# A macaron block on one core: the second expert layer as three 128-column products into the same PSUM columns

## The chip, the core and the metric

The kernel runs on one core of one Trainium2 chip. The time is that of one execution in microseconds (us); the runs of the kernel before gave 599.95, 600.19 and 601.44, median 600.19.
## The reference

For 8192 tokens of 128 numbers: a routed feed-forward layer, a gated scan over 512 steps, and the feed-forward layer again. The routed layer is

```
h = jnp.mod(x_flat[:, :TOP_K].sum(axis=1).astype(jnp.int32), E)
sel = jnp.stack([h, jnp.mod(h + 1, E)], axis=1)
def step(acc, params):
    e, W1e, b1e, W2e, b2e = params
    w = jnp.any(sel == e, axis=1).astype(x.dtype) / TOP_K
    y = jnp.maximum(x_flat @ W1e + b1e, 0.0) @ W2e + b2e
    return (acc + w[:, None] * y, None)
...
x = x + 0.5 * _L0_ffn_ref(_layernorm(x, axis=-1), L0_ffn_W1, L0_ffn_b1, L0_ffn_W2, L0_ffn_b2)
```

With E = 8 experts each token goes to its class's expert and the next one. W1 is 128 x 512 and W2 512 x 128 for each expert.

## The kernel before, in words

`ffn(r)` runs twice (r = 0 and 1), with the scan layer between. Each time, the tokens have been sorted by class, so that a tile of 256 tokens is gathered by two indirect DMAs and written back by two (the last tile has 128). There are 36 tiles per call. 25 are **pure**: all 256 tokens have one class. 11 are **mixed**: their two sub-blocks of 128 tokens may have different classes, so each has its own experts. The program has the order fixed: three pure tiles, then eleven times two pure and one mixed (`layout`).

- `layer1(tile, e)`, lines 745 to 759: for the expert e of two, four chunks of three matmuls. In a pure tile they have 256 columns, in a mixed tile each chunk is done twice with 128. The weights are the operand that is loaded into the array, `hi` and `lo`: two register adds for three matmuls.
- `layer2(tile, e)`, lines 761 to 779: for each chunk c and sub-block s, `hhi` (the high part of the hidden layer) is loaded and the columns `w` stream past it: 256, which are the weight's high and low half side by side. Then `hlo` is loaded, and `wh`, the high half, streams with 128. So Y has 256 columns per sub-block: the second half holds high x low. Both matmuls read the same register.
- `step(tile)`, lines 781 to 803: PE's order per iteration is layer1 of tile j for e = 0, the transposes of tile j + 1, layer2 of tile j - 1 for e = 0, layer1 of j for e = 1, layer2 of j - 1 for e = 1. In the last iteration that has a tile, layer1 for e = 1 comes ahead of layer2.
- `collect(tile)` on DVE, lines 1063 to 1070: O += scale x Y's first half, then, behind the semaphore `y_half`, O += scale x Y's second half. It stands behind `low` (lines 1043 to 1049), which makes the hidden layer's low part from ACT's high part (line 586).
- POOL gathers four tiles ahead and scatters three tiles behind (lines 498 to 509). Its scatters wait for `o_ready` of the collecting operation.

Of the kernel before, what the change touches and what calls it, by code (L numbers as in the profile page):

```python
# [17 lines left out]
ALU = mybir.AluOpType  # L18
# [4 lines left out]
P = 128  # L23
# [3 lines left out]
def macaron_kernel(nc, x, W_toP, W_U, W_F, W_V, W_lam, B_mat, C_mat, W_fromP, W1, b1, W2, b2, out):  # L27
# [6 lines left out]
    FT = 256  # L34
    SUB = FT // P
# [22 lines left out]
    with ExitStack() as ctx:  # L58
# [3 lines left out]
        def sem(name):  # L62
            return ctx.enter_context(nc.semaphore(name))
# [6 lines left out]

        ps = ctx.enter_context(nc.psum_tensor("ps", [P, 8, 512], F32))
        H = [ps[:, 2 * e:2 * e + 2, :].rearrange("p a (b n) -> p (a b) n", n=FT) for e in range(2)]
        Y = [ps[:, 4 + k, :].rearrange("p (s n) -> p s n", s=SUB) for k in range(2)]
        XTP = ps[:, 6, 0:FT]

# [25 lines left out]
        scl = scl_i[:].bitcast(F32)  # L102
# [58 lines left out]
        hhi = [[sb(f"hhi{k}{e}", [P, CH, FT], F16) for e in range(2)] for k in range(2)]  # L161
        hlo = [[sb(f"hlo{k}{e}", [P, CH, FT], F16) for e in range(2)] for k in range(2)]
# [82 lines left out]
        lo_done = [sem(f"lo_done{e}") for e in range(2)]  # L245
        res_done = sem("res_done")
        y_ready = sem("y_ready")
        y_half = sem("y_half")
        o_ready = sem("o_ready")
        scat = [sem(f"scat{k}") for k in range(SLOTS)]  # L250
        mxn0 = sem("mxn0")
# [413 lines left out]
        def _(pe):  # L665
# [74 lines left out]
            def ffn(r):  # L740
                load, held = table(PE_E, tab_w[:].rearrange("p j e -> p (j e)"), 2 * SUB, (E - 1) * WS), {}
                w1v = w1s[:].rearrange("p e f -> p (e f)")
                w2v = w2s[:].rearrange("p e c f -> p (e c f)")

                def layer1(tile, e):

                    pe.wait_ge(xlo_ready, tile.done())
                    if tile.j >= 1:
                        pe.wait_ge(lo_done[e], (tile + -1).done())
                    for s in range(1 if tile.pure else tile.subs):  # L750
                        at, tok = held[tile.j][2 * s + e], slice(0, FT) if tile.pure else slice(s * P, (s + 1) * P)
                        for c in range(CH):
                            hi = w1v[:, bass.ds(at + c * P, P)]
                            lo = w1v[:, bass.ds(at + DFF + c * P, P)]
                            o = H[e][:, c, tok]
                            nc.tensor.matmul(o, hi, xhi[tile.k][:, tok], start=True, stop=False)  # L756
                            nc.tensor.matmul(o, hi, xlo[tile.k][:, tok], start=False, stop=False)  # L757
                            ins = nc.tensor.matmul(o, lo, xhi[tile.k][:, tok], start=False, stop=True)  # L758
                    ins.then_inc(h_ready[e], 1)

                def layer2(tile, e):

                    pe.wait_ge(lo_done[e], tile.done())
                    if tile.r == 0 and tile.j == 0 and e == 0:
                        pe.wait_ge(w2_split, 2)
                    if e == 0 and tile.j >= 2:
                        pe.wait_ge(o_ready, (tile + -2).done())
                    for c in range(CH):
                        for s in range(tile.subs):
                            at, tok = held[tile.j][e if tile.pure else 2 * s + e], slice(s * P, (s + 1) * P)  # L770
                            w = w2v[:, bass.ds(at + c * 2 * P, 2 * P)]
                            wh = w2v[:, bass.ds(at + c * 2 * P, P)]
                            first = e == 0 and c == 0 and s == 0
                            nc.tensor.matmul(Y[tile.k][:, s, :], hhi[tile.k][e][:, c, tok], w,  # L774
                                             start=first, stop=False, skip_group_check=True)
                            ins = nc.tensor.matmul(Y[tile.k][:, s, 0:P], hlo[tile.k][e][:, c, tok], wh, start=False,  # L776
                                                   stop=(e == 1 and c == CH - 1), skip_group_check=True)
                    if e == 1:
                        ins.then_inc(y_ready, 1)

                def step(tile):
                    now, nxt, was = tile.valid(), (tile + 1).valid(), tile.j >= 1

                    early = tile.j == NJ - 1
                    if now:
                        layer1(tile, 0)
                    if nxt:
                        pe.wait_ge(xn_ready, (tile + 1).done())
                        if tile.j >= 0:
                            pe.wait_ge(xlo_ready, tile.done())  # L790
                        for s in range((tile + 1).subs):
                            ins = nc.tensor.transpose(XTP[:, s * P:(s + 1) * P], xn[(tile + 1).k][:, s, :], ident[:])  # L792
                        ins.then_inc(xt_ready, 1)
                    if tile.j == -1:
                        warm(5)
                    if early:
                        layer1(tile, 1)
                    if was:
                        layer2(tile + -1, 0)
                    if now and not early:  # L800
                        layer1(tile, 1)
                    if was:
                        layer2(tile + -1, 1)

                pe.wait_ge(table_ready, 1 + r)
                for j in range(-1, NJ + 1):
                    if 0 <= j < NJ:
                        held[j] = load(Tile(r, j).at)
                    step(Tile(r, j))
                    held.pop(j - 1, None)  # L810
# [68 lines left out]
        def _(dve):  # L879
            v = nc.vector  # L880
# [153 lines left out]
            def ffn(r):  # L1034
                load = table(DVE_E, tab_b2[:], SUB, (E - 1) * D)
                b2v = b2t[:].rearrange("p e d -> p (e d)")

                def x_low(tile):
                    dve.wait_ge(xhi_ready, tile.done())
                    c = slice(0, tile.cols)  # L1040
                    v.tensor_tensor(xlo[tile.k][:, c], XTP[:, c], xhi[tile.k][:, c], ALU.subtract).then_inc(xlo_ready, 1)  # L1041

                def low(tile, e):

                    dve.wait_ge(hi_done[e], tile.done())
                    c = slice(0, tile.cols)
                    v.scalar_tensor_tensor(out=hlo[tile.k][e][:, :, c], in0=H[e][:, :, c], scalar=0.0,  # L1047
                                           in1=hhi[tile.k][e][:, :, c], op0=ALU.max,
                                           op1=ALU.subtract).then_inc(lo_done[e], 1)

                def residual(tile):
                    at = load(tile.at)
                    if r == 0 and tile.j == 0:
                        dve.wait_ge(b2_ready, 1)
                    dve.wait_ge(gath[tile.slot], tile.moved())
                    if tile.j >= SLOTS:
                        dve.wait_ge(scat[tile.slot], (tile + -SLOTS).moved())
                    for s in range(tile.subs):
                        ins = v.tensor_tensor(O[tile.slot][:, s, :], G[tile.slot][:, s, 0:D],  # L1059
                                              b2v[:, bass.ds(at[0 if tile.pure else s], D)], ALU.add)  # L1060
                    ins.then_inc(res_done, 1)

                def collect(tile):
                    o, y = O[tile.slot][:, 0:tile.subs, :], Y[tile.k][:, 0:tile.subs, :]
                    dve.wait_ge(y_ready, tile.done())
                    v.scalar_tensor_tensor(out=o, in0=y[:, :, 0:P], scalar=scl[:, 2:3], in1=o, op0=ALU.mult,  # L1066
                                           op1=ALU.add).then_inc(y_half, 1)
                    dve.wait_ge(y_half, tile.done())
                    v.scalar_tensor_tensor(out=o, in0=y[:, :, P:2 * P], scalar=scl[:, 2:3], in1=o,  # L1069
                                           op0=ALU.mult, op1=ALU.add).then_inc(o_ready, 1)  # L1070

                x_low(Tile(r, 0))
                if r == 0:
                    w2_low(1)
                for j in range(NJ):
                    tile = Tile(r, j)
                    low(tile, 0)
                    if j + 1 < NJ:
                        x_low(tile + 1)
                    residual(tile)  # L1080
                    low(tile, 1)
                    if j >= 1:
                        collect(tile + -1)
                collect(Tile(r, NJ - 1))

            ffn(0)
# [119 lines left out]
```

## Time and profile before

| | |
|---|---|
| median of the runs | 600.19 us (599.95 to 601.44) |
| the profiled execution, first to last instruction (span) | 598.6 us |
| first call of ffn, about 61.5 to 262.6 us | 201 us |
| second call, about 385.5 to 584.7 us, and its last scatters | 199 us, and 14 us |
| PE busy | 514.1 us, 86% of the span |
| DVE busy | 432.9 us, 72% |

Of the profiled execution the page gives the span; its lowest run is 1.4 us longer, for what lies around the program. Matmuls are pipelined, and a matmul's row gives its own duration, longer than its place in the stream; what a matmul costs in a stream is the distance between the starts of two that follow each other. Sequencer rows are not counted as busy time, and PE's are listed only where a line of the program is asked for.

### The profile page before, as it was taken

The numbers are of one execution on the slowest core, as the hardware profiler recorded it, in microseconds if no ns is written. First come the engines' busy times: TensorE is split into PE (matmuls) and PEld (weight loads), VectorE is DVE, ScalarE is ACT, GpSimd is POOL, SyncE is SP. The second block draws the span as 40 slices with busy tenths as digits, with TensorE's granted clock in tenths as the row PEclk, the third lists the DMA queues.
The fourth block names the chain that finished last, engine by engine and source line by source line (L and its number), as shares of the span: only waits on it lengthen the run. The fifth ranks groups of instructions, "written<-read, shape, count | busy, mean of one in ns | idle before, by whom it ended". The sixth has DMA issues, their size and how long they took to land.

```text
span 598.6 us, 15962 instructions
## 1 busy us (share of the span) xinstructions
PE 514.1 (86%) x5269; PEld 437.2 (73%) x5269; DVE 432.9 (72%) x1026; ACT 296.2 (49%) x494; POOL 321.1 (54%) x410
## 2 busy tenths in 40 slices
PE   0278899999999999956799836999999999999990
PEld 0136599999999999942466614689999999999980
DVE  6899677777777777746876779677777777777760
ACT  2384655555555556412988400155555655555540
POOL 3014847777777767350016610447777677777543
PEclk9996999999999999997999967699999999999996
DMA  9980111112111112109003380111121111112100
GB/s 244 328 340 11 41 34 50 47 47 50 48 51 43 51 41 53 31 30 266 16 1 72 72 142 1 28 38 46 51 50 48 44 46 47 48 51 51 36 24 18
DMA packets 37850, 40.96 MB, mean 68 GB/s; under 512 B 5813, under 2 KB 30731, under 8 KB 37266
## 3 DMA queue, kind: packets, MB, share of 16 engines
q1 hardware_dynamic: 27698, 21.65, 13.5%
q0 software_dynamic: 9088, 17.87, 11.5%
q8 instruction: 51, 0.84, 0.6%
q10 hardware_dynamic: 992, 0.44, 0.3%
q14 instruction: 21, 0.17, 0.1%
HBM read 23.00 MB, written 17.83 MB: 68 GB/s over the span
## 4 chain that ended last, share of the span: by engine, by line
PE 69%; DVE 14%; issue 5%; DMA 3%; ACT 3%; POOL 3%; SPq 2%; POOLq 0%; DVEq 0%
PE ps L774 19%; PE ps L756 10%; PE ps L758 10%; PE ps L757 10%; PE ps L776 10%; PE ps L792 2%; SPq L366 2%; PE ps L680 2%; PE ps L728 2%; DMA X<-in_L_attn_x 1%; DVE X L1122 1%; DVE bn L1101 1%; POOL G L478 1%; DVE onehot_b L987 1%; PE ps L836 1%
## 5 line engine op out<-in xcount | busy, mean ns | idle before, releaser
L1047 DVE SCALAR_TENSOR_TENSOR hlo<-ps,hhi 128x1024 f16<-128x1024 f32 x144 | 174.1, 1209 | 103.0 <-ACT hhi L586 103.0
L586 ACT ACTIVATE hhi<-ps 128x1024 f16<-128x1024 f32 x144 | 145.7, 1012 | 170.1 <-PE ps L758 170.1
L774 PE MATMUL ps<-w2s,hhi 128*128 x1136 | 202.3, 273 | 0.0
L776 PE MATMUL ps<-w2s,hlo 128*128 x1136 | 194.9, 219 | 0.0
L478 POOL DMA_INDIRECT G<-rows,places x142 | 141.9, 1000 | 88.2 <-issue 40.2
L756 PE MATMUL ps<-xhi,w1s 128*128 128x256 f16 (+1 forms) x736 | 168.0, 248 | 3.9 <-DVE xlo L1041 2.1
L758 PE MATMUL ps<-xhi,w1s 128*128 128x256 f16 (+1 forms) x736 | 168.0, 248 | 0.0
L757 PE MATMUL ps<-xlo,w1s 128*128 128x256 f16 (+1 forms) x736 | 167.9, 248 | 0.0
L774 PEld LDWEIGHTS ps<-w2s,hhi 128*128 128x128 f16 x1136 | 111.1, 98 | 12.1
L776 PEld LDWEIGHTS ps<-w2s,hlo 128*128 128x128 f16 x1136 | 111.1, 98 | 1.3
L486 POOL DMA_INDIRECT x1d<-O,places x71 | 71.3, 1004 | 41.6 <-issue 29.1
L486 POOL DMA_INDIRECT out<-O,places x71 | 71.3, 1004 | 40.3 <-issue 26.8
L600 ACT ACTIVATE xn<-G 128x127 f32<-128x127 f32 x142 | 62.0, 489 | 50.0 <-DMA G<-rows,places 50.0
L756 PEld LDWEIGHTS ps<-xhi,w1s 128*128 x736 | 72.0, 98 | 11.2 <-issue 6.0
L758 PEld LDWEIGHTS ps<-xhi,w1s 128*128 x736 | 72.0, 98 | 4.7
L757 PEld LDWEIGHTS ps<-xlo,w1s 128*128 x736 | 72.0, 98 | 3.4
L680 PE MATMUL ps<-ones_row,ones 128*128 128x512 f16 x111 | 32.7, 459 | 11.7 <-DMA X<-x1d 11.0
L1066 DVE SCALAR_TENSOR_TENSOR O<-ps,scl_i,O 128x256 f32<-128x256 f32 x72 | 34.0, 472 | 3.6 <-PE ps L776 3.6
L1069 DVE SCALAR_TENSOR_TENSOR O<-ps,scl_i,O 128x256 f32<-128x256 f32 x72 | 34.6, 481 | 2.5
L680 PEld LDWEIGHTS ps<-ones_row,ones 128*128 128x128 f16 x111 | 12.7, 116 | 29.6 <-issue 21.7
L1059 DVE TENSOR_TENSOR O<-G,b2t 128x128 f32<-128x128 f32 x142 | 34.3, 282 | 0.0
L1041 DVE TENSOR_TENSOR xlo<-ps,xhi 128x256 f16<-128x256 f32 x72 | 29.5, 410 | 2.6 <-ACT xhi L592 2.6
(240 smaller groups left out, 509.5 us busy)
## 6 DMA issues: line engine op xcount, KB each, us to landing
rows<-X SPq DMA_DIRECT2D x2, 2080.0 KB, 12.0
rows<-X SPq DMA_DIRECT2D x4, 1040.0 KB, 7.6
X<-in_L_attn_x SPq DMA_DIRECT2D x8, 512.0 KB, 8.0
X<-x1d SPq DMA_DIRECT2D x8, 512.0 KB, 7.4
G<-rows,places POOLq DMA_INDIRECT x142, 2.6
w1r<-in_L_ffn_W SPq DMA_DIRECT2D x1, 2048.0 KB, 11.3
x1d<-O,places POOLq DMA_INDIRECT x71, 2.3
out<-O,places POOLq DMA_INDIRECT x71, 2.3
```

The source lines that it names most:

```text
L478: nc.gpsimd.indirect_dma_start(out=G[tile.slot][:, s, :], out_offset=None, in_=rows, in_offset=bass.IndirectOffsetOnAxis(ap=places[:, tile ...
L486: nc.gpsimd.indirect_dma_start(out=dst, out_offset=bass.IndirectOffsetOnAxis(ap=places[:, tile.at, SUB + s:SUB + s + 1], axis=0), in_=O[ti ...
L586: nc.scalar.activation(hhi[tile.k][e][:, :, 0:tile.cols], H[e][:, :, 0:tile.cols], ACT.Relu).then_inc(hi_done[e], 1)
L600: ins = nc.scalar.activation(xn[tile.k][:, s, 0:D - 1], g[:, s, 0:D - 1], ACT.Identity, bias=g[:, s, D:D + 1], scale=g[:, s, D + 1:D + 2])
L680: nc.tensor.matmul(ps[:, bank, :], ones16[:], ones_row[:], start=True, stop=True)
L756: nc.tensor.matmul(o, hi, xhi[tile.k][:, tok], start=True, stop=False)
L757: nc.tensor.matmul(o, hi, xlo[tile.k][:, tok], start=False, stop=False)
L758: ins = nc.tensor.matmul(o, lo, xhi[tile.k][:, tok], start=False, stop=True)
L774: nc.tensor.matmul(Y[tile.k][:, s, :], hhi[tile.k][e][:, c, tok], w, start=first, stop=False, skip_group_check=True)
L776: ins = nc.tensor.matmul(Y[tile.k][:, s, 0:P], hlo[tile.k][e][:, c, tok], wh, start=False, stop=(e == 1 and c == CH - 1), skip_group_check ...
L1047: v.scalar_tensor_tensor(out=hlo[tile.k][e][:, :, c], in0=H[e][:, :, c], scalar=0.0, in1=hhi[tile.k][e][:, :, c], op0=ALU.max, op1=ALU.sub ...
L1069: v.scalar_tensor_tensor(out=o, in0=y[:, :, P:2 * P], scalar=scl[:, 2:3], in1=o, op0=ALU.mult, op1=ALU.add).then_inc(o_ready, 1)
```

## The change

`layer2` no longer streams 256 columns past `hhi`. It loads `hhi` and streams the high half (128 columns), loads `hlo` and streams the high half, loads `hhi` again and streams the low half. All three add into the same 128 columns, so Y has 128 columns per sub-block, and `collect` is one operation. `y_half` is gone.

```
-        Y = [ps[:, 4 + k, :].rearrange("p (s n) -> p s n", s=SUB) for k in range(2)]
+        Y = [ps[:, 4 + k, 0:FT].rearrange("p (s n) -> p s n", s=SUB) for k in range(2)]
...
-                            w = w2v[:, bass.ds(at + c * 2 * P, 2 * P)]
                             wh = w2v[:, bass.ds(at + c * 2 * P, P)]
+                            wl = w2v[:, bass.ds(at + c * 2 * P + P, P)]
                             first = e == 0 and c == 0 and s == 0
-                            nc.tensor.matmul(Y[tile.k][:, s, :], hhi[tile.k][e][:, c, tok], w,
-                                             start=first, stop=False, skip_group_check=True)
-                            ins = nc.tensor.matmul(Y[tile.k][:, s, 0:P], hlo[tile.k][e][:, c, tok], wh, start=False,
+                            y = Y[tile.k][:, s, :]
+                            nc.tensor.matmul(y, hhi[tile.k][e][:, c, tok], wh, start=first, stop=False,
+                                             skip_group_check=True)
+                            nc.tensor.matmul(y, hlo[tile.k][e][:, c, tok], wh, start=False, stop=False,
+                                             skip_group_check=True)
+                            ins = nc.tensor.matmul(y, hhi[tile.k][e][:, c, tok], wl, start=False,
                                                    stop=(e == 1 and c == CH - 1), skip_group_check=True)
...
-                    v.scalar_tensor_tensor(out=o, in0=y[:, :, 0:P], scalar=scl[:, 2:3], in1=o, op0=ALU.mult,
-                                           op1=ALU.add).then_inc(y_half, 1)
-                    dve.wait_ge(y_half, tile.done())
-                    v.scalar_tensor_tensor(out=o, in0=y[:, :, P:2 * P], scalar=scl[:, 2:3], in1=o,
-                                           op0=ALU.mult, op1=ALU.add).then_inc(o_ready, 1)
+                    v.scalar_tensor_tensor(out=o, in0=y, scalar=scl[:, 2:3], in1=o, op0=ALU.mult,
+                                           op1=ALU.add).then_inc(o_ready, 1)
```

PE, start of layer 2 of a mixed tile, in the kernel before. ps is PSUM, w2s the second layer's weights, and a MATMUL row stands for a weight load and a matmul:

```order
L792 MATMUL ps<-ident,xn 128x128 [waits xlo_ready,xn_ready]
L792 MATMUL ps<-ident,xn 128x128
L774 REGISTER_ALU [waits o_ready,lo_done0]
L774 MATMUL ps<-w2s,hhi 128x256
L776 MATMUL ps<-w2s,hlo 128x128
L774 REGISTER_ALU
```

The same place in the changed kernel:

```order
L794 MATMUL ps<-ident,xn 128x128 [waits xlo_ready,xn_ready]
L794 MATMUL ps<-ident,xn 128x128
L774 REGISTER_ALU [waits o_ready,lo_done0]
L774 MATMUL ps<-w2s,hhi 128x128
L776 MATMUL ps<-w2s,hlo 128x128
L778 REGISTER_ALU
L778 MATMUL ps<-w2s,hhi 128x128
L774 REGISTER_ALU
```

The third product's address has a register add of its own: two adds per chunk and sub-block where there was one.

PE, the first chunk of layer 2 of a pure tile, before, where both sub-blocks share the chunk's add:

```order
L774 REGISTER_ALU [waits o_ready,lo_done0]
L774 MATMUL ps<-w2s,hhi 128x256
L776 MATMUL ps<-w2s,hlo 128x128
L774 MATMUL ps<-w2s,hhi 128x256
L776 MATMUL ps<-w2s,hlo 128x128
L774 REGISTER_ALU
```

And now:

```order
L774 REGISTER_ALU [waits o_ready,lo_done0]
L774 MATMUL ps<-w2s,hhi 128x128
L776 MATMUL ps<-w2s,hlo 128x128
L778 REGISTER_ALU
L778 MATMUL ps<-w2s,hhi 128x128
L774 MATMUL ps<-w2s,hhi 128x128
L776 MATMUL ps<-w2s,hlo 128x128
L778 MATMUL ps<-w2s,hhi 128x128
L774 REGISTER_ALU
```

Here too each chunk has two adds for one. Over the program, layer 2's REGISTER_ALU rows go from 736 to 1472 and its matmuls (each with its load) from 2272 to 3408; the 1472 ISA rows of layer 1 and the waits on PE are as they were.

DVE, a tile's collecting operation between two `low`, before (O is the tile's output, scl the scale):

```order
L1047 SCALAR_TENSOR_TENSOR hlo<-ps,hhi 128x1024 [waits hi_done1]
L1066 SCALAR_TENSOR_TENSOR O<-ps,scl_i,O 128x256 [waits y_ready]
L1069 SCALAR_TENSOR_TENSOR O<-ps,scl_i,O 128x256 [waits y_half]
L1047 SCALAR_TENSOR_TENSOR hlo<-ps,hhi 128x1024 [waits hi_done0]
L1041 TENSOR_TENSOR xlo<-ps,xhi 128x256 [waits xhi_ready]
```

And now:

```order
L1049 SCALAR_TENSOR_TENSOR hlo<-ps,hhi 128x1024 [waits hi_done1]
L1068 SCALAR_TENSOR_TENSOR O<-ps,scl_i,O 128x256 [waits y_ready]
L1049 SCALAR_TENSOR_TENSOR hlo<-ps,hhi 128x1024 [waits hi_done0]
L1043 TENSOR_TENSOR xlo<-ps,xhi 128x256 [waits xhi_ready]
```

One of the two operations and the wait between them are gone; nothing else on DVE moved.

## Rows read from the trace of the kernel before

**Rows 1.** First section of the page: busy us (share of the span), instructions.

```profile
PE 514.1 (86%) x5269; PEld 437.2 (73%) x5269; DVE 432.9 (72%) x1026; ACT 296.2 (49%) x494; POOL 321.1 (54%) x410
```

**Rows 2.** Busy time by stretch (the two ffn calls), with the granted clock behind POOL.

```profile
61.50:264.50 203.00, 198.06 (x2317) 182.17 (x2316) 147.37 (x253) 109.78 (x178) 136.78 (x136) 1.00 0.17 44
386.50:585.00 198.50, 196.30 (x2311) 181.68 (x2309) 143.85 (x250) 108.57 (x176) 131.69 (x133) 1.00 0.17 45
```

**Rows 3.** Waits: who waited for whom, us in total, times, longest.

```profile
PE ps L756 <- DVE xlo L1041: 2.1, 2, 1.3
PE ps L756 <- DVE hlo L1047: 1.7, 3, 0.6
```

**Rows 4.** Groups by shape: count, busy us, mean ns of one, idle before.

```profile
L774 PE MATMUL ps<-w2s,hhi 128*128 x1136 | 202.3, 273 | 0.0
...
L1069 DVE SCALAR_TENSOR_TENSOR O<-ps,scl_i,O 128x256 f32<-128x256 f32 x70 | 33.9, 484 | 2.5
```

**Rows 5.** Timeline of PE, 202.5 to 209: start us, us; each stage's first matmul.

```profile
202.75 0.27 PE L774 MATMUL ps<-w2s,hhi 128*128 x1
...
204.07 0.27 PE L756 MATMUL ps<-xhi,w1s 128*128 128x256 f16 x1
...
205.38 0.27 PE L774 MATMUL ps<-w2s,hhi 128*128 x1
...
206.70 0.22 PE L756 MATMUL ps<-xhi,w1s 128*128 128x128 f16 x1
...
208.04 0.39 PE L792 MATMUL ps<-ident,xn 128*128 128x128 f32 x2
```

**Rows 6.** Timeline of weight loads, 579 to 580, first load of each chunk.

```profile
579.31 0.10 PEld L756 LDWEIGHTS ps<-xhi,w1s 128*128 x1 [0.74 <-issue]
...
579.56 0.10 PEld L756 LDWEIGHTS ps<-xhi,w1s 128*128 x1
...
579.80 0.10 PEld L756 LDWEIGHTS ps<-xhi,w1s 128*128 x1
```

**Rows 7.** Lines 774, 756, 304: sequencer rows, ns min/median/max, first to last start us.

```profile
L774 PEldq ALU_OP  x736: 32/32/42, 69.9 to 582.9; - x184
...
L756 PEldq FUSED_REGOPS  x736: 42/46/46, 62.9 to 580.1; - x184
...
L304 PEldq TENSOR_LOAD <-tab_w x72: 327/331/521, 61.6 to 576.4; - x72
```

**Rows 8.** Line 774, sequencer, 518.35 to 519.16: eight adds in a row.

```profile
L774 PEldq ALU_OP  x8: 32/32/32, 518.4 to 519.2; - x8
```

**Rows 9.** Lines 304, 749, 756, sequencer: the start of an iteration at 411.5.

```profile
L304 PEldq TENSOR_LOAD <-tab_w x1: 332/332/332, 411.5 to 411.5; - x1
...
L749 PEldq EVENT_SEMAPHORE  x1: 51/51/51, 411.9 to 411.9; - x1
...
L756 PEldq FUSED_REGOPS  x1: 42/42/42, 412.0 to 412.0; - x1
```

**Rows 10.** Line 756 and PE's timeline, 408.9 to 410.45: adds ahead of their matmuls.

```profile
L756 PEldq FUSED_REGOPS  x4: 42/46/46, 409.0 to 409.8; - x4
L756 PEld LDWEIGHTS ps<-xhi,w1s x1: 98/98/98, 410.3 to 410.3; 128*128 x1
...
409.06 0.27 PE L774 MATMUL ps<-w2s,hhi 128*128 x1
...
410.32 0.22 PE L776 MATMUL ps<-w2s,hlo 128*128 x1
```

**Rows 11.** Timelines of POOL and DVE at the end of the program.

```profile
581.40 0.98 POOL L486 DMA_INDIRECT out<-O,places  x1 [1.52 <-PE ps L758]
...
589.13 0.98 POOL L486 DMA_INDIRECT out<-O,places  x1 [0.31 <-issue]
...
585.08 0.35 DVE L1069 SCALAR_TENSOR_TENSOR O<-ps,scl_i,O 128x128 f32<-128x128 f32 x1
```

**Rows 12.** Busy time by stretch, in the scan layer; PE first, then PEld, DVE, ACT, POOL.

```profile
280.00:340.00 60.00, 54.60 (x349) 35.35 (x346) 45.63 (x190) 48.43 (x95) 19.22 (x68) 1.00 0.26 59
```

More of the change, by code:

```diff
@@ L247, in macaron_kernel @@
         y_ready = sem("y_ready")
-        y_half = sem("y_half")
         o_ready = sem("o_ready")
```

## The prediction

 The waits confirm it: over the program PE waits 3.8 us for DVE's low parts (2.1 + 1.7, five times) [rows 3], so DVE's 72% is not a limit. The ffn calls last as long as PE takes.
>
> What PE takes is the distance of matmul starts. The timeline gives three prices [rows 5]. Layer 2: 8 pairs (256 and 128 columns) from 202.75 to 204.07, 0.165 us a pair. Layer 1 of a pure tile: 12 matmuls of 256 columns from 204.07 to 205.38, 0.109 each. Layer 1 of a mixed tile: 24 matmuls of 128 columns from 206.70 to 208.04, 0.0558 each, every one with its own weight load. So loads are hidden behind 128 columns too.
>
> A second view has to be read, since PE's stream is fed by a sequencer that also does the register adds: 736 ALU_OP for layer 2, 1472 FUSED_REGOPS for layer 1 (736 for each of two lines), 72 TENSOR_LOADs [rows 7]. What an add takes there shows where nothing is queued. Near the end, after a wait, layer 1 of a mixed tile runs at one chunk per 0.245 us (579.31, .56, .80) [rows 6], though its three matmuls need 0.167. A chunk has two adds: **0.123 to 0.124 us per FUSED_REGOPS**. Its matmuls and loads add nothing visible. In layer 2 eight ALU_OPs stand in 0.8 us, seven steps: **0.114 us per ALU_OP** [rows 8], with two matmuls and their loads between. An iteration's TENSOR_LOAD and first wait take 0.5 us (411.5 to 412.0) [rows 9]; the other three waits 0.1 each, as the one from 411.9 to 412.0: 0.8 in all.
>
> This sequencer runs ahead, and a queue holds what it has handed over. How far: the adds of layer 1 run at 409.0, the load of the first of these matmuls at 410.3, and between them PE starts the 16 matmuls from 409.06 to 410.32 [rows 10]. I take 16 matmuls as the queue's depth.
>
> **The change part by part.**
>
> *Streamed columns.* As many as before (384), but in three matmuls: 3 x 0.0558 = 0.1674 against 0.165, so 0.0024 to 0.0026 more for each of 1136 groups [rows 4, 5]: **+2.9 us**, all on the path, since PE is it. That the three add into the same columns costs nothing: layer 1 of a mixed tile does the same at 0.0558.
>
> *One collecting operation less.* 0.48 us of DVE in each of 70 tiles, a bit less in two [rows 4]. What PE waits for on DVE is 3.8 us, at starts and ends of the calls [rows 3]; those waits end with `low` and `x_low`, at stage ends where `collect` comes behind them. At the program's end POOL's seven scatters, released by layer 1 of the last tile (581.40), follow each other to 589.13, while the last collecting operation starts at 585.08 [rows 11], 4 us ahead of the scatter that needs it; the first call ends alike. **0**, between 0 and -3.8.
>
> *Register adds.* 736 ALU_OPs more, one for `wl` per chunk (pure) or chunk and sub-block (mixed). They cost nothing while the sequencer keeps its lead. So the budget of a round of three tiles (two pure, one mixed), which the program repeats:
> - PE: layer 1 two pure tiles x 24 x 0.109 = 5.24, one mixed 48 x 0.0558 = 2.68; six transposes at a matmul's 0.109, 0.66; layer 2 three tiles x 16 x 0.1674 = 8.04 (before 7.92). **16.6 us** (before 16.5).
> - Sequencer: 16 + 16 + 32 = 64 FUSED_REGOPS x 0.124 = 7.94; ALU_OPs before 8 + 8 + 16 = 32 x 0.114 = 3.65, now 64, 7.30; three iterations x 0.8 = 2.4. Before **14.0**, now **17.6 us**.
>
> Before, the sequencer had 2.5 us to spare per round. Now it is 1.0 us short: it becomes the bound. Twice ten full rounds (the eleventh ends with the half tile) lose at least 20.4 us.
>
> More is lost, because lead beyond 16 matmuls (16 x 0.0558 = 0.89 us) can't be stored. I walk through a round, PE's time less the sequencer's, with L the lead. Layer 1 mixed: 1.34 - 1.98; pure: 1.31 - 0.99; layer 2 mixed: 1.34 - 1.82; pure: 1.34 - 0.91.
> - Mixed tile's layer 1, with the pure tile's layer 2. L = 0.89. e = 0: entry 0.5 and layer 1, -1.14: stall 0.25, L = 0; layer 2 +0.43. e = 1: -0.74: stall 0.31; +0.43.
> - Next, pure layer 1, mixed layer 2. e = 0: entry and layer 1 -0.18, L = 0.25; -0.48: stall 0.23. e = 1: +0.22, -0.48: stall 0.26, L = 0.
> - Then both pure. e = 0: entry 0.5 with nothing queued: stall 0.5; layer 1 +0.32, layer 2 +0.43. e = 1: +0.22, +0.43 makes 1.40, cut to 0.89.
>
> Sum 1.55 us per round, x 20 = **+31 us**. Bounds: 20 us if the lead is never cut. If ALU_OP's price is at the low end of what the rounded row allows (0.7 us for seven steps, 0.100), the round is short by 0.1 alone; with two thirds of the 0.5 us that the walk loses at the full queue that makes 0.45, 9 us. If a second add in a group costs as much as a FUSED_REGOPS, 0.124, a round loses 0.64 more: 44 us. I take 31, by the row that is the same operation in the same line.
>
> Sum: 2.9 + 0 + 31 = **+34 us** on a span of 598.6, and as much on the median 600.19: **634 us**.
>
> One page states a depth for this queue: the Trainium skill, "TensorE: Matmul & The Clock Gate", in its table ahead of the first section, gives TensorE 64 entries, which would be 32 matmuls with their loads; rows 10 show 16, and the measurement is what I go by. By the page's depth no lead is cut, and the sum is 2.9 + 20.4, 623 us.
>
> **The rivals.**
> - *The sequencer keeps up, and PE's stream alone decides.* So if the adds really overlap each other where matmuls are short. For it: no row before has two adds with a single matmul behind the second in layer 2. Against it: layer 1's chunk has exactly that pattern in rows 6, at 0.124 per add. It needs ALU_OP under (16.6 - 7.9 - 2.4) / 64 = 0.098. Then 600.2 + 2.9 = 603.1.
> - *Not slower: DVE's relief pays.* Same condition, under 0.098 per add, and then the 3.8 us of PE's waits for DVE [rows 3] must shrink, because `low` is issued half a microsecond earlier. At the most 600.2 + 2.9 - 3.8 = 599.3. Against it: these waits stand where no `collect` is ahead.
> - *Short matmuls with loads are slower than the rows say.* In a stream of load and matmul, 0.081 us each for 128 columns instead of 0.0558: 1136 x (3 x 0.081 - 0.165) = 88, 688 us. Against it: 24 in a row at 0.0558 [rows 5]. The figure is that of the Trainium skill, same page, section "Back-to-back issue gap"; this trace disagrees.
> - *The clock falls, since PE now stalls inside the stage.* One mixed tile at 1.2 GHz costs some 96 matmuls x 0.056 = 5 us, 20 of them 100 us: 734. Against it: the scan layer, where PE has gaps (54.6 of 60 us busy) [rows 12], keeps 1.00 from 280 to 340.
> - *The change doesn't do what it says*, the adds being shared: the order of the built program shows the 736 new ones. No chance.
>
> **How the numbers follow.** Sequencer-bound, 634: 0.85, of which 0.79 lies between 612 (9 + 2.9) and 648 (44 + 2.9). Deeper queue, 623: 0.04, inside as well. Stream alone, 603.1: 0.05. DVE's relief, 599.3: 0.04. Slow pairs 0.01, clock 0.01. Range 612 to 648, which holds 0.83. A measurement of this kernel can tell about 0.3%, 1.8 us: 603.1 is slower. Faster 0.02, the same 0.02 (the relief's two halves), slower 0.96.
>
> **What would show it.** ALU_OP of layer 2 1472 times, in mixed tiles with steps of about 0.11; layer 2 of a mixed tile no longer at 0.167 per group but towards 0.23, and layer 1 of a mixed tile towards 0.25 per chunk; a hole in PE of some 0.5 us at the start of the iteration behind a mixed tile's layer 2; both ffn calls longer by 15 to 19 us each and nothing else changed; the collecting operation at 0.48 us once per tile, DVE's busy time 36 us less; clock 1.00 in both calls. I am wrong if pure and mixed tiles alike run without holes (the adds are cheaper than I read), or if the third product's start is later than 0.056 behind the second in pure tiles too, where there is lead (a price of same columns or of loads).

## The result and the profile after

The changed kernel takes 651.06 us (649.71 to 651.08) beside 600.17 us (599.95 to 601.44) for the kernel before on the same chip: a ratio of 1.084, interval 1.0825 to 1.0856. It is slower, as forecast, but by 51 us instead of 34, and 3 us above the range.

The first section of its page (busy us, share of the span, instructions) answers to [rows 1]:

```profile
PE 556.5 (86%) x6405; PEld 468.4 (72%) x6405; DVE 398.7 (61%) x954; ACT 296.2 (46%) x494; POOL 321.4 (50%) x410
```

PE has 1136 matmuls more, DVE 72 operations and 34.2 us less. The span is 649.1 us, 50.5 more than before. The two ffn calls, which answer to [rows 2] (length, then PE, PEld, DVE, ACT, POOL, and behind them the granted clock):

```profile
61.50:289.10 227.60, 218.28 (x2886) 196.66 (x2884) 130.10 (x217) 109.75 (x178) 136.94 (x136) 1.00 0.15 40
...
411.00:637.00 226.00, 217.95 (x2885) 197.47 (x2884) 127.34 (x215) 108.93 (x178) 133.63 (x136) 1.00 0.16 40
```

Each call is longer by some 25 us (the forecast was 15 to 19), and the clock in both is 1.00 as before. PE counts as busy for 96% of either window (98 and 99% before), which looks like a PE that still sets the pace. It doesn't: a matmul's row lasts 0.22 us, so a next one that starts 0.1 us late leaves no idle time. Steps between starts have to be read, and the sequencer's rows. Those of layer 2 are at line 774 and at line 778, the third product, which the change gave an add of its own (count, ns min/median/max, first and last start):

```profile
L774 PEldq ALU_OP  x736: 32/32/42, 69.8 to 634.7; - x184
...
L778 PEldq ALU_OP  x736: 32/32/32, 70.0 to 634.8; - x184
```

So 1472 adds, as forecast. What they do to layer 2 of a mixed tile stands in the timeline of weight loads (start us, duration us), first load of each group:

```profile
504.24 0.10 PEld L774 LDWEIGHTS ps<-w2s,hhi 128*128 128x128 f16 x1
...
504.46 0.10 PEld L774 LDWEIGHTS ps<-w2s,hhi 128*128 128x128 f16 x1
...
504.69 0.10 PEld L774 LDWEIGHTS ps<-w2s,hhi 128*128 128x128 f16 x1
...
504.91 0.10 PEld L774 LDWEIGHTS ps<-w2s,hhi 128*128 128x128 f16 x1
...
505.19 0.10 PEld L774 LDWEIGHTS ps<-w2s,hhi 128*128 128x128 f16 x1
...
505.42 0.10 PEld L774 LDWEIGHTS ps<-w2s,hhi 128*128 128x128 f16 x1
```

A group takes 0.225 us, two adds at 0.113, where its three matmuls need 0.167. One step is 0.28 instead of 0.225: it holds a pause of about 0.055. That pause is what the prediction lacked.

The waits (who waited for whom, us in total, times, longest) have the two rows of [rows 3] unchanged, and a new one: twenty holes of 0.4 us at the start of an iteration, where layer 1's first matmul finds an empty queue. They hold 8 us of the loss; most of it stands in no row of waits.

```profile
PE ps L755 <- issue: 8.2, 20, 0.4
PE ps L755 <- DVE xlo L1043: 2.1, 2, 1.3
PE ps L755 <- DVE hlo L1049: 1.7, 3, 0.6
```

The length of a round of three tiles can be read from the table loads, one per iteration: 25 of them span eight rounds. Before, and then after (line, sequencer, operation, count, ns, first and last start):

```profile
L304 PEldq TENSOR_LOAD <-tab_w x25: 327/331/335, 428.0 to 560.0; - x25
```

```profile
L303 PEldq TENSOR_LOAD <-tab_w x25: 328/329/334, 456.9 to 608.6; - x25
```

132.0 / 8 = 16.50 us a round before, 151.7 / 8 = 18.96 after. Twenty rounds of 2.46 us are 49 of the 50.5 us.

### The profile page after: what moved, and what is told of

The parts are those of the page before. It is cut to its first block, busy times and chain, and to the rows that moved or that the text cites. A ratio compares the mean times of both kernels' runs of the same rounds, so it can differ in the third digit from the quotient of the medians.

```text
span 649.1 us, 18898 instructions
## 1 busy us (share of the span) xinstructions
PE 556.5 (86%) x6405; PEld 468.4 (72%) x6405; DVE 398.7 (61%) x954; ACT 296.2 (46%) x494; POOL 321.4 (50%) x410
## 4 chain that ended last, share of the span: by engine, by line
PE 71%; DVE 13%; issue 5%; DMA 3%; ACT 3%; POOL 2%; SPq 2%; POOLq 0%; DVEq 0%
PE ps L755 13%; PE ps L774 11%; PE ps L757 10%; PE ps L778 10%; PE ps L776 10%; PE ps L756 9%; PE ps L794 3%; SPq L365 2%; PE ps L727 1%; PE ps L679 1%; DMA X<-in_L_attn_x 1%; DVE X L1121 1%; DVE bn L1100 1%; POOL G L477 1%; DVE onehot_b L989 1%
## 5 line engine op out<-in xcount | busy, mean ns | idle before, releaser
L776 PE MATMUL ps<-w2s,hlo 128*128 x1136 | 204.6, 219 | 0.0
L774 PE MATMUL ps<-w2s,hhi 128*128 x1136 | 204.4, 218 | 0.1
L778 PE MATMUL ps<-w2s,hhi 128*128 x1136 | 204.4, 218 | 0.0
L755 PE MATMUL ps<-xhi,w1s 128*128 128x256 f16 (+1 forms) x736 | 177.2, 251 | 12.5 <-issue 8.2
L757 PE MATMUL ps<-xhi,w1s 128*128 128x256 f16 (+1 forms) x736 | 177.4, 250 | 0.0
L756 PE MATMUL ps<-xlo,w1s 128*128 128x256 f16 (+1 forms) x736 | 175.5, 248 | 0.0
L774 PEld LDWEIGHTS ps<-w2s,hhi 128*128 128x128 f16 x1136 | 110.6, 97 | 6.3 <-issue 0.3
L778 PEld LDWEIGHTS ps<-w2s,hhi 128*128 128x128 f16 x1136 | 110.7, 97 | 0.0
L1068 DVE SCALAR_TENSOR_TENSOR O<-ps,scl_i,O 128x256 f32<-128x256 f32 x72 | 34.0, 472 | 4.8 <-PE ps L778 4.8
```

The costliest lines, as they stand in the source:

```text
L774: nc.tensor.matmul(y, hhi[tile.k][e][:, c, tok], wh, start=first, stop=False, skip_group_check=True)
L776: nc.tensor.matmul(y, hlo[tile.k][e][:, c, tok], wh, start=False, stop=False, skip_group_check=True)
L778: ins = nc.tensor.matmul(y, hhi[tile.k][e][:, c, tok], wl, start=False, stop=(e == 1 and c == CH - 1), skip_group_check=True)
```

## The experiments

The theory: the 736 new adds make the sequencer the bound, with a lead of 16 matmuls at the most, and it pauses besides. Rivals: the streamed columns or the weight loads of short matmuls, a deeper queue, the collecting operation.

**The new adds taken out.** Of the changed kernel, with the low half of `w2` read at a fixed address (so the output is of other weights):

```
-                            wl = w2v[:, bass.ds(at + c * 2 * P + P, P)]
+                            wl = w2v[:, c * 2 * P + P:(c + 1) * 2 * P]
```

> The changed kernel, but the third product reads its low weight half at a fixed address (expert 0), so it needs no register add: 736 adds in layer 2 instead of 1472, all matmuls, loads and the single collecting operation as in the changed kernel. The low half is then that of the wrong expert. Sequencer theory (the added register adds are what costs): per round of three tiles the sequencer needs 7.9 + 3.6 + 2.4 us and some 1 us of pauses, 15 us, against PE's 16.6, so PE bounds again and only its stream is left: 600.2 + 2.9 = 603 us (602 to 605). Rival (a third load and matmul per group, or three products into the same columns, cost it): the adds change nothing, about 651 us.

Measured: 613.11 us, ratio 1.0207 (1.0192 to 1.0221). So 38 of the 51 us go with the adds, but 10 more than the streamed columns stay. The timeline of PE shows where, in layer 1 of a mixed tile behind layer 2 of a pure one (first matmuls of chunks, some left out; start us, duration us):

```profile
504.28 0.22 PE L774 MATMUL ps<-w2s,hhi 128*128 x1
...
504.44 0.22 PE L755 MATMUL ps<-xhi,w1s 128*128 128x128 f16 x1
...
505.11 0.22 PE L755 MATMUL ps<-xhi,w1s 128*128 128x128 f16 x1
...
505.33 0.23 PE L755 MATMUL ps<-xhi,w1s 128*128 128x128 f16 x1
...
505.58 0.23 PE L755 MATMUL ps<-xhi,w1s 128*128 128x128 f16 x1
...
505.98 0.23 PE L755 MATMUL ps<-xhi,w1s 128*128 128x128 f16 x1
...
506.24 0.41 PE L794 MATMUL ps<-ident,xn 128*128 128x128 f32 x2
```

Four chunks run at 0.167 us (504.44 to 505.11), then 0.22, 0.25, 0.40 (a pause of 0.15 is in the last): the stored lead is used up, and PE follows layer 1's own adds. Before, the same stage ran its eight chunks at 0.167 [rows 5], with the same adds. What differs is the lead ahead of it: 16 matmuls of 128 columns are 16 x 0.0558 = 0.89 us of work, 16 in pairs of 256 and 128 are 8 x 0.165 = 1.32. A queue that counts matmuls stores less time when they are cut in pieces. That is a second cost of the change, apart from its adds. The run with both low halves fixed, below, tests it.

**The adds alone.** Of the kernel before, with 256 and 128 columns and both collecting operations; the second product reads the low half through a register of its own in place of the high one:

```
-                            wh = w2v[:, bass.ds(at + c * 2 * P, P)]
+                            wh = w2v[:, bass.ds(at + c * 2 * P + P, P)]
```

> The kernel before, two matmuls of 256 and 128 columns and two collecting operations, with one edit: the second matmul reads the low half of the weight instead of the high half, by an address of its own, so layer 2 has 1472 register adds instead of 736. It computes the wrong product there. Sequencer theory: the adds alone bring nearly all of the loss. Per round the sequencer needs 7.9 + 7.2 + 2.4 + 0.9 (17 pauses of 0.055 us, one per 32 instructions), 18.5 us, a little less than in the changed kernel, which has 96 instructions more per round: 644 to 649 us. Rival (third product costs): 600.2 us, as before.

Measured: 641.61 us, ratio 1.0686 (1.0666 to 1.0705), a bit under the bounds given. Adds with nothing else cost 41 us, though PE's stream is that of before. The twenty holes are here as well:

```profile
PE ps L756 <- issue: 8.2, 20, 0.5
```

**The middle product left out.** The changed kernel without the product of `hlo` and the high half; adds as in the changed kernel, PE with a third less to stream in layer 2:

```
-                            nc.tensor.matmul(y, hlo[tile.k][e][:, c, tok], wh, start=False, stop=False,
-                                             skip_group_check=True)
```

> The changed kernel without the middle product (low part of the hidden layer times the high half): two matmuls of 128 columns and two register adds per group; that term is left out of the result. PE's stream is 1136 x 0.056 = 63 us shorter than in the changed kernel. Sequencer theory: the sequencer's program is that of the kernel before with the adds alone, so the time is the same as there, 644 to 649 us, and only the pauses of 96 instructions less per round (3 x 0.055 us x 20 = 3.4 us) come off the 651. Rival (PE's stream or its loads bound): 651 - 63 = 588 us or less.

Measured: 638.09 us, ratio 1.063 (1.0607 to 1.0654). A PE with 1136 matmuls less is 13 us faster than in the changed kernel and 38 slower than before: PE's stream is not what decides, which the rival at 588 needed. What is left is the sequencer's own time, nearly bare.

**One collecting operation.** The kernel before with its second collecting operation (the low columns' sum) left out:

```
                     v.scalar_tensor_tensor(out=o, in0=y[:, :, 0:P], scalar=scl[:, 2:3], in1=o, op0=ALU.mult,
-                                           op1=ALU.add).then_inc(y_half, 1)
-                    dve.wait_ge(y_half, tile.done())
-                    v.scalar_tensor_tensor(out=o, in0=y[:, :, P:2 * P], scalar=scl[:, 2:3], in1=o,
-                                           op0=ALU.mult, op1=ALU.add).then_inc(o_ready, 1)
+                                           op1=ALU.add).then_inc(o_ready, 1)
```

> The kernel before with one collecting operation: the second one, which adds the second half of Y, is left out with its wait (that term is missing from the result). Theory: DVE is not on the path, 599.5 to 600.5 us. Rival (DVE's relief shortens PE's waits): up to 3.8 us less, 596.4.

Measured: 600.71 us, ratio 0.9999 (0.9989 to 1.0009). Its page has DVE at 398.8 us for 432.9 [rows 1]:

```profile
PE 515.8 (86%) x5269; PEld 438.5 (73%) x5269; DVE 398.8 (67%) x954; ACT 296.2 (49%) x494; POOL 321.5 (54%) x410
```

34 us of DVE are worth nothing, as the prediction had it.

**The adds of one kind of tile.** With the pause in the budget and the queue at 16 matmuls, the round was walked again, and two runs were forecast from it: the fixed address in pure tiles alone, and in mixed tiles alone.

```
-                            wl = w2v[:, bass.ds(at + c * 2 * P + P, P)]
+                            lo = c * 2 * P + P
+                            wl = w2v[:, lo:lo + P] if tile.pure else w2v[:, bass.ds(at + lo, P)]
```

> The changed kernel with the third product's register add left out in pure tiles alone (its low half there comes from expert 0, the wrong one): 400 of the 736 added adds are gone, 336 stay, all in mixed tiles. Lead theory (adds cost where the lead is already used up; lead beyond 16 queued matmuls is lost; one pause per 32 instructions): a round loses 0.5 us at the mixed tile's layer 1 and 0.9 us in the iteration after it, 1.4 us x 20 + 2.9: 631 us. Rival (each added add costs the same wherever it stands: 51 us less the 2.9 of streaming, by 336/736): 600.2 + 2.9 + 22 = 625 us.

Measured: 630.74 us, ratio 1.0504 (1.0489 to 1.0519). The other run has `if not tile.pure` in that line:

> The counterpart: the third product's add is left out in mixed tiles alone (wrong expert's low half there); the 400 in pure tiles stay. Lead theory: the mixed tile's layer 1 stands beside a pure tile's layer 2, which now gives back 0.35 us instead of 0.8 per half, so it loses 0.45 + 0.59 us, and the next iterations nothing: 1.04 us x 20 + 2.9, 624 us, less than with the 336 in mixed tiles though more adds stay. Rival (same price everywhere): 600.2 + 2.9 + 26 = 629 us, more than there.

Measured: 623.99 us, ratio 1.0393 (1.0378 to 1.0408). Both as walked. Of the new adds 400 are in pure tiles and 336 in mixed ones. A pure tile has PE work to hide them (a half's 1.31 + 1.34 us against 0.99 + 0.91 of adds), a mixed tile has none (1.34 + 1.34 against 1.98 + 1.82): taking the 336 away gives 27 us, the 400 only 20. The holes at an iteration's start go with the mixed tiles' adds: with pure tiles fixed they are still there,

```profile
PE ps L755 <- issue: 7.9, 20, 0.4
```

and with mixed tiles fixed the waits have no such row.

**A short middle product.** The changed kernel with eight columns of the middle product in place of 128: all instructions of the changed kernel, little of its streaming.

```
-                            nc.tensor.matmul(y, hlo[tile.k][e][:, c, tok], wh, start=False, stop=False,
+                            nc.tensor.matmul(y[:, 0:8], hlo[tile.k][e][:, c, tok], wh[:, 0:8], start=False, stop=False,
```

> The changed kernel with the middle product cut to 8 of its 128 columns (the rest of the term is missing): the sequencer's program, instruction by instruction, and the weight loads are those of the changed kernel, PE's stream is up to 57 us shorter. Against the kernel without the middle product (638.1) it has 2 x 1033 instructions more and no add more. Theory of pauses (0.06 us per 32 instructions): 64 pauses, 4 us: 642 us. If a pause is not a matter of the number of instructions: 638 us. If what the changed kernel takes beyond that one is PE's stream or the weight loads: 651 us.

Measured: 641.30 us, ratio 1.0684 (1.0668 to 1.0701). 9.8 us below the changed kernel: so much of its 51 is not the sequencer's own time, but lead that can't be stored once PE's stream is longer. The 3.2 us above the run without the product I then read as pauses that come with the instructions; that reading fell, below, so that the forecast of 642 came near by luck.

**Layer 1 of mixed tiles without its low half's adds too.** On top of the first experiment, in mixed tiles:

```
-                            lo = w1v[:, bass.ds(at + DFF + c * P, P)]
+                            lo = w1v[:, bass.ds(at + DFF + c * P, P)] if tile.pure else w1v[:, DFF + c * P:DFF + (c + 1) * P]
```

> The kernel with the third product's low half at a fixed address (613.1 us, 12.5 over the kernel before, of which 2.9 are the streamed columns), and besides it the low half of layer 1's weights in mixed tiles at a fixed address (expert 0): 336 register adds fewer in layer 1 of mixed tiles, no matmul changed. Those terms are of the wrong expert. Lead theory (the other 9.6 us are stalls in layer 1 of mixed tiles, since 16 queued matmuls of 128 columns hold 0.89 us of work instead of 1.32): the stalls go, 603 us (602 to 605). Rival (a price of the third product anywhere else): stays at 613.

Measured: 603.19 us, ratio 1.0047 (1.0032 to 1.0062). The number of adds in layer 1 falls by 336, as the edit says (168 of layer 2's are listed as FUSED_REGOPS here). The 10 us of the first experiment were layer 1 of mixed tiles running out of lead. What is left is the streamed columns, +3.0 us (1.9 to 3.7) for the +2.9 of the prediction; with the sequencer out of the way PE's row fills its calls (first call: 199.95 us busy for 198.06 in [rows 2]):

```profile
61.00:268.00 207.00, 199.95 (x2890) 190.34 (x2888) 131.11 (x217) 110.33 (x180) 139.31 (x138) 1.00 0.17 45
```

**What the pause goes by.** Up to here I took it for one pause in 32 instructions of PE's program (adds, loads and matmuls together), since a group of layer 2 and a chunk of layer 1 have eight each and the pauses stood four groups apart. Where groups have six instructions, as without the middle product, the traces didn't fit that. So layer 1's product with the low part of x was left out as well, which leaves two adds, two loads and two matmuls in every chunk of layer 1, and for each chunk and sub-block of a mixed tile's layer 2 (in a pure tile both sub-blocks share the two adds):

```
-                            nc.tensor.matmul(o, hi, xlo[tile.k][:, tok], start=False, stop=False)
```

> Taken away here: the middle product of layer 2 as in the run without it, and of layer 1 the product with the low part of x, so that every chunk of both layers is two adds, two loads and two matmuls (six instructions); the 1472 + 1472 adds, the table loads and the waits are as in the changed kernel. Two theories of the sequencer's pause. (a) It comes once per 32 instructions of PE's program, as I have said so far: a round of three tiles has 475 instructions here instead of 539 without layer 2's middle product alone, so 14.8 pauses of 0.058 us instead of 16.8, 0.12 us less per round, 20 rounds: 638.1 - 2.3 = 635.8 us; in the trace the pauses stand every 5.3 chunks. (b) It comes once per eight of the sequencer's own register operations (the adds, the table loads and one further step per iteration: 128 + 6 = 134 per round), whatever matmuls and loads lie between; this is what a closer reading of the traces so far gives. Then a round has 16.75 pauses as before, 18.6 us, and nothing changes: 638.1 us (637 to 639), and in the trace the pauses stand every four chunks, in both layers.

Measured: 636.31 us, ratio 1.0585 (1.0562 to 1.0609). Its timeline of weight loads in layer 1 of a pure tile and layer 2 of a mixed one, one load behind each add (start us, duration us):

```profile
476.76 0.10 PEld L756 LDWEIGHTS ps<-xhi,w1s 128*128 x1
476.93 0.10 PEld L755 LDWEIGHTS ps<-xhi,w1s 128*128 x1
...
477.59 0.10 PEld L773 LDWEIGHTS ps<-w2s,hhi 128*128 128x128 f16 x1
477.70 0.10 PEld L775 LDWEIGHTS ps<-w2s,hhi 128*128 128x128 f16 x1
477.86 0.10 PEld L773 LDWEIGHTS ps<-w2s,hhi 128*128 128x128 f16 x1
...
478.54 0.10 PEld L773 LDWEIGHTS ps<-w2s,hhi 128*128 128x128 f16 x1
478.65 0.10 PEld L775 LDWEIGHTS ps<-w2s,hhi 128*128 128x128 f16 x1
478.85 0.10 PEld L773 LDWEIGHTS ps<-w2s,hhi 128*128 128x128 f16 x1
```

Steps are 0.11 to 0.12; the long ones (0.17, 0.16, 0.20) end at 476.93, 477.86 and 478.85, and from each to the next are eight loads, so eight adds and 24 instructions. The pause goes by the sequencer's register operations, eight at a time; how many matmuls and loads lie between doesn't count. With the starts of all adds, table loads and waits in the trace: in the middle of both calls of this run and of the one without the middle product a gap of over 15 ns beyond an operation's usual step stands at nine in ten or more of the eighths and nowhere else, if the adds and the table loads are counted and one further step per iteration (the wait ahead of the transposes, which takes 0.126 us where others take 0.106). The time alone speaks for the other reading: 636.3 (634.4 to 637.2 by the ratio's interval) agrees with its 635.8 and not with 638.1. The rhythm in the trace decides against it, and most of the missing time lies in the size of the pauses: their mean is 0.053 us here and 0.058 in the run without the middle product, which makes 0.08 us for 16.75 of them, and a round takes 18.51 us instead of 18.58, 1.4 us of the 1.8 in twenty rounds.

## Why the prediction was right on the mechanism and wrong on its size

**What held.** The adds are the cause (run alone: 41 us; taken out of the changed kernel: 38 us less). The prices per add: 0.113 for ALU_OP and 0.124 for FUSED_REGOPS, as [rows 8] and [rows 6] gave them. The streamed columns: +3.0 us, forecast +2.9, and the starts of three products into the same columns are 0.05 to 0.06 us apart:

```profile
508.50 0.22 PE L774 MATMUL ps<-w2s,hhi 128*128 x1
508.56 0.22 PE L776 MATMUL ps<-w2s,hlo 128*128 x1
508.61 0.22 PE L778 MATMUL ps<-w2s,hhi 128*128 x1
509.22 0.28 PE L755 MATMUL ps<-xhi,w1s 128*128 128x256 f16 x1 [0.40 <-issue]
```

so the rival of slow pairs is out; in the first experiment's layer 2 of a pure tile, where PE had lead, the step is 0.0558. The collecting operation: 0. The clock: 1.00 in both calls though PE had holes. The signs in the profile: layer 2 of mixed tiles at 0.225 us a group, a hole of 0.4 us at an iteration's start (the last row above), twenty in all, DVE 34 us less (36 forecast).

**What failed.** The term of the sum "Sequencer: ... Before 14.0, now 17.6 us". It was too small by a pause that it lacked. Per round 128 adds, three table loads and three of the longer waits are 134 operations, 134 / 8 = 16.75 pauses; their mean is 0.058 us in the run without the middle product and 0.066 in the changed kernel (worked out from the starts of the sequencer's rows; most are between 0.02 and 0.09, some 0.15). That is 1.0 to 1.1 us, so a round needs 18.6 to 18.7 us of the sequencer instead of 17.6, 2.0 to 2.1 more than PE's 16.6 instead of 1.0. The loss by the full queue comes on top, as the prediction said, with about 0.3 us instead of its 0.5: 18.96 measured. By the walk below the pause makes 18.95 of 18.21, 0.74 us a round: 15 of the 17 us that the forecast was short.

The walk itself, step by step through a round, stands. Done again after the runs, with 0.0558, 0.109 and 0.165 us for PE, 0.1125, 0.124, 0.106 (wait), 0.126 and 0.39 us (table load) for the sequencer, 16 matmuls for the queue and 0.058 us at every eighth operation, it gives the round of each kernel (the right column from 25 table loads in the second call, as above; the first column has no pause and 16 matmuls, the second the pause and 32):

| kernel | no pause, 16 | pause, 32 | pause, 16 | measured |
|---|---|---|---|---|
| before | 16.48 | 16.48 | 16.49 | 16.50 |
| after | 18.21 | 18.61 | 18.95 | 18.96 |
| low half fixed | 16.92 | 16.60 | 17.08 | 17.10 |
| adds alone | 17.69 | 18.61 | 18.61 | 18.59 |
| fixed in pure tiles | 17.50 | 16.70 | 18.04 | 18.04 |
| fixed in mixed tiles | 17.30 | 16.70 | 17.68 | 17.68 |
| no middle product | 17.64 | 18.61 | 18.61 | 18.58 |
| middle of 8 columns | 17.88 | 18.61 | 18.63 | 18.69 |
| both low halves fixed | 16.60 | 16.60 | 16.60 | 16.62 |
| two products each | 17.64 | 18.61 | 18.61 | 18.51 |

Without the pause the changed kernel has 1.73 us a round over before, 35 us in twenty rounds: the forecast. Neither other column fits all rows; with both terms every round is met within 0.1 us, most within 0.03. One pause length, that of the run without the middle product, serves for all; with the changed kernel's own mean of 0.066 the walk gives 19.05 us for it, 0.09 too much, perhaps because some of what its rows show at an eighth operation is waiting for the full queue. The pause costs before nothing, since its sequencer has 2.5 us to spare.

**It could have been seen.** The timeline behind [rows 6] goes on, in the trace of before:

```profile
580.19 0.10 PEld L756 LDWEIGHTS ps<-xhi,w1s 128*128 x1 [0.16 <-issue]
```

0.39 us after the load at 579.80 instead of 0.245, with nothing that it could wait for. I took the two even steps as the price and left the next one out.

**The rivals.** Stream alone (603.1) is what the kernel takes once no add is late (603.19), so it was priced rightly and its condition not met. The deeper queue is excluded: at 32 matmuls the low half at a fixed address would cost 16.60 a round, and it took 17.10, 136.8 / 8 from its table loads:

```profile
L303 PEldq TENSOR_LOAD <-tab_w x25: 327/331/335, 435.1 to 571.9; - x25
```

The rows show the depth directly, too. Counted at every add and table load of seven rounds, in eight of the kernels, the matmuls that the sequencer has handed over and PE has not started are never more than 17; they are 17 again and again in the six whose lead fills up, before and after among them. The Trainium skill, "TensorE: Matmul & The Clock Gate", in its table ahead of the first section, gives 64 entries; these runs fit 16 matmuls, 32 instructions with their loads.

**Expectations that missed.** For the low half at a fixed address I expected 603, from the sums of a round alone (15 us of the sequencer against PE's 16.6). I didn't walk that round: with 16 matmuls of 128 columns it takes 16.92 instead of 16.60 without any pause, and 17.08 with it, since shorter matmuls also shorten the lead for adds that were there before. The adds alone came out some 3 us under their bounds: those were set near the changed kernel's own loss, but a queue of 256- and 128-column matmuls holds 1.32 us, and the walk loses nothing there by a full queue (18.61 with 16 or with 32). The run without the middle product was held to the same bounds, less 3.4, and took 638.1; the 3.5 us between it and the adds alone lie outside the full rounds (18.58 and 18.59).

**What stays open.** What the pause is: only its rhythm and size were shown, in profiled runs. Its size varies, and its mean is smaller where less lies between the adds (0.066 us in the changed kernel, 0.060 with the short middle product, or 0.064 with the few pauses that stand one step late, at a wait, 0.058 without the product, 0.053 with two products each); so the 3.2 us between the second and third of these are partly this (0.11 us a round), partly the first rounds of each call; why, no run settled.

## What to carry to other kernels

Cutting a matmul into shorter ones with run-time addresses costs twice beside its columns: each new address is an add on PE's sequencer (0.11 to 0.12 us here, twice what a matmul of 128 columns takes), and a queue that counts matmuls then holds less time for the adds that were there already. Make the sequencer's budget per round of the schedule, from an average over a long stretch that shows it bare and not from its even steps, and walk it against PE with the queue's depth; a surplus in a round's sum doesn't tell that no stage runs dry. A busy share of 96% on PE doesn't tell that PE is the bound: its rows overlap, so compare the steps between starts with the best steps of the same form.

## What the hardware showed that was not expected

PE's sequencer pauses after every eighth register operation (adds, table loads), 0.05 to 0.07 us on the mean, at most about 0.15, however many matmuls and loads lie between; a round that is bound by the sequencer pays 0.9 to 1.1 us in 18.5 to 19.0 for it. That is how the traces show it; what it is, no run settled.

The rows of these operations don't show their price: an ALU_OP's row lasts 32 ns, and the next comes 113 ns later. The Trainium skill, "Perfetto Trace Analysis", section "Sequencer-only Instruction (DRAIN, etc)", says that the profile of such an instruction holds its execution alone, not the waiting before it or what follows. The trace agrees: 81 of 113 ns lie outside the row.
